# Two cross-attention layers on one core: maxima of the next block taken in the bank of the projections, keys and values computed at other places, and unread products on TensorE

## The reference

```python
q = split_heads(LN(x) @ Wq.T + bq) / sqrt(16)      # 16 heads of 16, 128 queries
k = split_heads(ctx @ Wk.T + bk)                   # 12544 keys
v = split_heads(ctx @ Wv.T + bv)
s = q @ k.T + (1 - mask) * -10000                  # first layer only: mask (128, 12544)
x = x + softmax(s) @ v                             # the second layer has another projection Wo, bo
```

## Time and profile before

| | |
|---|---|
| Median of 3 runs | 1091.87 us (1090.59 to 1091.94) |
| The profiled execution: time | 1094.2 us |
| The profiled execution: span, first to last instruction | 1092.5 us |
| TensorE busy | 1024.6 us, 94% of the span |
| VectorE busy | 743.1 us, 68% |
| ScalarE busy | 679.3 us, 62% |
| GpSimd busy | 420.0 us, 38%, nearly all in the first layer |
| Mean granted clock of TensorE | 0.975 |

### The profile page before, as it was taken

One profiled execution on the slowest core, in us unless ns is written; L12 is line 12 of the kernel. 1 busy time (PEld: TensorE's weight loads), 2 busy tenths in 40 slices (PEclk: granted clock), 3 DMA queues, 4 the chain that ended last, 5 costly groups with the idle time before them and its releaser, 6 DMA issues. The chain is left out here.

```text
span 1092.5 us, 30637 instructions
## 1 busy us (share of the span) xinstructions
PE 1024.6 (94%) x12851; PEld 687.2 (63%) x12851; DVE 743.1 (68%) x1714; ACT 679.3 (62%) x951; POOL 420.0 (38%) x374
## 2 busy tenths in 40 slices
PE   7899999999999999977878899999999999999877
PEld 4466666666666666655544576666666666666655
DVE  4788888888888888766347756655656555556555
ACT  3677777777778787765542555555655556555632
POOL 4268888888888888760100000000000000000000
PEclk9899999999999999998987999999999999999998
DMA  7410122201222012130031010111100111000000
GB/s 305 137 59 29 52 69 69 69 19 52 69 70 69 19 53 69 52 133 22 10 134 49 2 32 6 35 36 36 35 15 22 36 35 36 2 2 2 2 1 6
DMA packets 14682, 53.31 MB, mean 49 GB/s; under 512 B 3025, under 2 KB 4817, under 8 KB 13649
## 3 DMA queue, kind: packets, MB, share of 16 engines
q1 hardware_dynamic: 14544, 51.35, 13.6%
HBM read 51.21 MB, written 0.13 MB: 47 GB/s over the span
## 5 line engine op out<-in xcount | busy, mean ns | idle before, releaser
L740 DVE TENSOR_REDUCE tile_max<-ps_max 128x1 f32<-128x448 f32 x416 | 241.9, 620 | 161.1 <-PE ps_max L1054 159.7
L737 DVE CUSTOM_DVE_ANT_0 unread<-ps_max,masks 128x448 bf16<-128x448 f32 x432 | 253.5, 621 | 70.6 <-PE ps_max L1054 68.5
L413 POOL TENSOR_TENSOR probs<-probs,masks 128x512 f32<-128x512 f32 x182 | 227.8, 1273 | 77.9 <-ACT probs L526 76.9
L533 ACT ACTIVATE probs<-probs 128x1024 f32<-128x1024 f32 x196 | 207.4, 1058 | 58.7 <-DVE probs L795 46.7
L538 ACT ACTIVATE probs<-ps_scores 128x1024 f32<-128x1024 f32 x193 | 187.2, 1021 | 90.4 <-PE ps_scores L1095 90.3
L1095 PE MATMUL ps_scores<-q_pad,k_full 32*128 32x256 f32 x3088 | 233.9, 380 | 0.0
L1111 PE MATMUL ps_out<-probs,values 128*32 128x128 f32 x6272 | 214.9, 278 | 6.0 <-ACT probs L533 4.9
L1111 PEld LDWEIGHTS ps_out<-probs,values 128*32 128x32 f32 x6272 | 161.4, 111 | 58.8 <-issue 50.1
L1054 PE MATMUL ps_max<-k_high,q_high 32*128 32x448 bf16 x848 | 183.7, 360 | 14.0 <-DVE tile_max L740 7.6
L1095 PEld LDWEIGHTS ps_scores<-q_pad,k_full 32*128 32x128 f32 x3088 | 193.8, 188 | 1.0
L1042 PE MATMUL ps_proj<-ctx_t,wk 128*128 128x448 f32 x368 | 163.4, 567 | 0.0
(11 more groups left out here) (249 smaller groups left out, 787.7 us busy)
## 6 DMA issues: line engine op xcount, KB each, us to landing
ctx_t<-in_ctx_t SPq DMA_DIRECT2D x28, 896.0 KB, 5.3
masks<-in_mask_n SPq DMA_DIRECT2D x14, 448.0 KB, 3.4
masks<-in_mask_t SPq DMA_DIRECT2D x14, 448.0 KB, 3.6
room_w<-in_L_attn_f_w SPq DMA_DIRECT2D x2, 1024.0 KB, 8.9
room_w<-in_L_ffn_w SPq DMA_DIRECT2D x2, 1024.0 KB, 7.5
room_w<-in_L_ffn_w_gate SPq DMA_DIRECT2D x1, 1024.0 KB, 10.4
room_w<-in_L_ffn_w_up SPq DMA_DIRECT2D x1, 1024.0 KB, 12.9
room_w<-in_L_ffn_w_down SPq DMA_DIRECT2D x1, 1024.0 KB, 14.9
```

Of the source, the lines that this page charges most:

```text
L413: nc.gpsimd.tensor_tensor(p, p, three(mask_t[m % 2], TILES)[:, t, :].unsqueeze(1).to_broadcast([P, 4, P]), ALU.add).then_inc(sig("bias_add ...
L533: nc.scalar.activation(prob(T, half), prob(T, half), ACT.Exp).then_inc(sig(f"exp_done{half}"), 1)
L737: ins = v.tensor_tensor_reduce(unread[:, j % 2, :], max_bank(m, j)[:, 0:HALF], mask_n[m % 2][:, HALF * half:HALF * (half + 1)], 1.0, -3e38 ...
L740: ins = v.tensor_reduce(tile_max[:, h, half:half + 1], ps_max[:, j % 2, 0:HALF], AX_X, ALU.max)
```

## The change

**Maxima.** `ps_proj` becomes a third bank for them: where two stand behind the scores, the first goes to `ps_proj` (except at t = 1, where the sums are turned in it), all others take the banks of `ps_max` in turn. A table (`MAX_BANK`, `MAX_AFTER`) holds the bank of each and how many maxima must have been read before. In the blocks that are not the first of a layer, the counts change from 1 (t = 0, 2, 3, 4) or 0 behind the scores and 2 at every t behind the weighing, to 2 behind the scores (1 at t = 1, in the first layer at t = 3 also) and 2 behind the weighing at t = 1, 3, 5 only (1 at t = 5 in the second layer). The sum stays 32. Ahead of the next scores stand 2 as before.

**VectorE's order in the first layer:** the first maximum behind the scores, then the mask's addition, then the second.

**Keys and values.** The keys of block 14 move from the stage between the layers into block 12; one piece of values of block 15 stays beside the first maxima, the other three go between the layers, in another order.

**The gated feed-forward** is done in two halves (SiLU and the product with up), and SiLU's table is loaded ahead by a dummy activation.

**Unread products** are added: small ones at the start, 2 and 4 ahead of `turn_max` of a layer's first block, one behind each of ten pairs of maxima, one per tile from t = 2 in block 13 and 3 behind it, and 3 in the feed-forward.

```diff
-        EXTRA_AT = (0, 2, 3, 4)
-        LAST_AT = 5
+
+
+        ONE_AT = ((1, 3), (1,))
+        WEIGHED_AT = ({1: 2, 3: 2, 5: 2}, {1: 2, 3: 2, 5: 1})
+        LAST_AT, SUMS_AT = 5, 1
         def count_at(m, t):
-            n = m % NB
...
             now, ahead = (0, 0, 0), (0, 0, 0)
+            first, middle = 1 if t in ONE_AT[l] else 2, WEIGHED_AT[l].get(t, 0)
             if n + 1 < NB:
-                if t < LAST_AT:
-                    now = (2 if n == 0 else int(t in EXTRA_AT), 2, 2)
-                elif t == LAST_AT:
-                    now = (0, 2, 0)
+                if n == 0:
+                    now = (2, 2, 2) if t < LAST_AT else (0, 2, 0) if t == LAST_AT else now
+                elif t <= LAST_AT:
+                    now = (first, middle, 2 if t < LAST_AT else 0)
             if n + 2 < NB:
-                ahead = (0, 0, 2) if t == LAST_AT else (0, 2, 2) if t > LAST_AT else (0, 0, 0)
+                ahead = (0, 0, 2) if t == LAST_AT else (first, middle, 2) if t > LAST_AT else ahead
             return now, ahead
-        MAXIMA = {}
+
+        MAXIMA, MAX_BANK, MAX_AFTER = {}, {}, {}
...
+            done, read = {NB * l: 2 * H}, {bank: 2 * H * (NB * l + 1) for bank in range(2)}
+            turn_of = 0
             for m in range(NB * l, NB * (l + 1)):
                 for t in range(TILES):
...
                             here += [(to, j) for j in range(at, at + count)]
                             done[to] = at + count
+                        for i, (to, j) in enumerate(here):
+                            if k == 0 and len(here) == 2 and i == 0 and (t != SUMS_AT or m % NB == 0):
+                                MAX_BANK[to, j] = 2
+                            else:
+                                MAX_BANK[to, j], MAX_AFTER[to, j] = turn_of, read[turn_of]
+                                read[turn_of] = 2 * H * to + j + 1
+                                turn_of = 1 - turn_of
...
         def max_bank(m, j):
-            return (ps_max[:, j % 2, :], ps_scores[:, j % 2, :])[1 - j // 2 % 2 if m == 0 else 0]
-
-        def max_reuse(m):
-            return 4 if m == 0 else 2
+            if m == 0:
+                return (ps_max[:, j % 2, :], ps_scores[:, j % 2, :])[1 - j // 2 % 2]
+            return (ps_max[:, 0, :], ps_max[:, 1, :], ps_proj)[MAX_BANK[m, j]]
...
-        BETWEEN = [("k", NB, j) for j in range(4)] + [("k", NB + 1, j) for j in range(4)]
-        BETWEEN += [("v", NB, u) for u in range(PAIRS)] + [("k", NB + 2, j) for j in range(3)]
...
-        BESIDE = [("k", NB + 2, 3)] + [("v", NB + 1, u) for u in range(PAIRS)]
-        BESIDE_AT = (1, 4, 7, 10, 13)
+        BETWEEN = [("k", NB + 1, 0), ("k", NB + 1, 1), ("v", NB, 0), ("v", NB, 1), ("k", NB + 1, 2), ("v", NB, 2), ("k", NB + 1, 3),
+                   ("k", NB + 2, 0), ("v", NB, 3), ("v", NB + 1, 0), ("v", NB + 1, 1), ("v", NB + 1, 2)]
+        BETWEEN += [("k", NB + 2, 1), ("k", NB + 2, 2)]
+
+
+        BESIDE = [("k", NB + 2, 3), ("v", NB + 1, 3)]
+        BESIDE_AT = (1, 4)
         def keys_in_block(m):
-            return m < BLOCKS and m not in (NB, NB + 1, NB + 2)
+            return m < BLOCKS and m not in (NB + 1, NB + 2)
...
+                    act.wait_ge(sig("table_loaded"), 2)
+                    nc.scalar.activation(stat[:, 30:31], ones[:, 0:1], ACT.Silu).then_inc(sig("table_loaded"), 1)
...
-                    act.wait_ge(sig("gate_ready"), 1)
-                    nc.scalar.activation(gelu, ps_scores[:, 0:2, :].rearrange("p a n -> p (a n)"), ACT.Silu,
-                                         scale=stat[:, 20:21]).then_inc(sig("silu_ready"), 1)
-                    between_out(10, 11, 12, 13)
+                    for half in range(2):
+                        act.wait_ge(sig("gate_ready"), half + 1)
+                        nc.scalar.activation(gelu[:, 512 * half:512 * (half + 1)], ps_scores[:, half, :], ACT.Silu,
+                                             scale=stat[:, 20:21]).then_inc(sig("silu_ready"), 1)
...
-                        for k, j in behind_scores:
+                        for k, j in behind_scores[0:1 + l]:
                             maximum(k, j)
                         if l == 0 and is_last(m):
                             bias_last(m, t)
                         elif l == 0:
                             bias_first(m, t)
+                        for k, j in behind_scores[1 + l:]:
+                            maximum(k, j)
                         if t == SUMS_AT and n > 0:
                             add_sums(m - 1)
...
+                    for half in range(2):
+                        cols = slice(512 * half, 512 * (half + 1))
+                        dve.wait_ge(sig("gate_ready"), 3 + half)
+                        dve.wait_ge(sig("silu_ready"), 1 + half)
+                        note(v.scalar_tensor_tensor(out=big[:, cols], in0=ps_scores[:, 2 + half, :], scalar=stat[:, 21:22],
+                                                    in1=gelu[:, cols], op0=ALU.mult, op1=ALU.mult))
+                    dve.wait_ge(sig("dve_link"), links[0])
...
-                need("max_free", J + 1 - max_reuse(m))
+                if m == 0:
+                    need("max_free", J - 3)
+                elif MAX_BANK[m, j] == 2:
+                    proj_free(("max_free", J + 1))
+                else:
+                    pe.wait_ge(sig("max_free"), MAX_AFTER[m, j])
...
             pe.wait_ge(sig("idents"), 3)
+            idents(4)
...
                 if l == 0:
+                    idents(4)
...
                             beside_in(BESIDE_AT.index(i))
-                    for u in range(len(BESIDE)):
-                        beside_read(u)
+                        elif i > 5:
+                            idle_products(1, ps_out)
+                        if i == 5:
+                            for u in range(len(BESIDE)):
+                                beside_read(u)
                 read_by[0] = ("max_copied", NB * l + 1)
+                idle_products(2 + 2 * l, ps_proj)
...
+                        if m == NB - 1 and t > SUMS_AT:
+                            proj_free(None)
+                            idle_products(1, ps_proj)
                         for k, j in ahead:
                             maximum(k, j)
+                if l == 0:
+                    idle_products(3, ps_proj)
...
+                            last.then_inc(sig("gate_ready"), 1)
+                    between_in(10, 11, 12)
+                    idle_products(1, ps_proj)
...
+                    idle_products(2, ps_proj)
...
```

28 lines of the change are left out of this document (14 added, 14 removed).

## The result

The changed kernel takes 1098.86 us in the median, the kernel before, on the same chip, 1091.91. The ratio of their runs is 1.0055, 95% interval 1.0040 to 1.0069: 6 us slower by the ratio, 7 by the medians, where the forecast said 1095.8 and 3.9. The profiled execution took 1098.86 us with a span of 1097.1, the one of before 1094.2 and 1092.5.

What follows compares the result with a forecast made beforehand. TensorE was taken to bound the first layer, with VectorE close behind. Terms from +14.7 (blocks 1 to 11) to -6.4 (second layer) sum to +3.9 on 1091.87, giving 1095.8 us; own range 1091 to 1101, with rivals 1078 to 1107.

Steps and rivals of the forecast that it cites:

- t = 5 of the first layer: TensorE waits for a bank read only behind the mask; lent values begin at 4.25 instead of 2.87, +1.38 us a block.
- the wait isn't there: Rival: the bank at t = 5 is free in time, 1063 us; wait smaller or absent has chance 0.18.
- t = 6: First layer: turned maxima wait for a mask one maximum later, from 2.96 to 3.50 after the pair, +0.54 us.
- t = 1: First layer: a maximum comes ahead of the sums' addition and the values wait for that addition, +0.39 us.
- t = 0, 2, 4: First-layer tiles: the pair behind the weighing goes, worth 0.29, and the second maximum costs 0.02; -0.27 us each.
- Block 0: All five full tiles get the wait of t = 5, a tile of keys 5.96 instead of 4.92; +5.3 us.
- Blocks 12 and 13: Block 12's waits and half-clock stretches filled by keys, -1.5 us; block 13's products +0.9 against a faster clock, 0.
- Between the layers: SiLU in halves -1.2 us, shorter waits at the first pair maxima -2.5, low-clock slices 19 and 21 -1.5.
- Block 14's scores: Second layer's start: scores of 2.20 us at 1.2 GHz take about 1.1 at full clock, half counted, -1.5 us.
- The second layer: No mask stands between the reads; -0.53 us a block, -6.4 for twelve; block 26 -1.5, block 14 0.
- Clock lost: Rival: new waits at t = 5 and t = 6 bring the first layer's clock down; +12, 1108 us, chance 0.17.
- Clock gained: Rival: unread products and the filled block 12 keep the clock at 2.4 GHz from 440 on; 1088 us, chance 0.23.

Runs made afterwards that it cites:

- experiment 5: Changed kernel with one first-layer maximum moved from behind the scores at t = 5 to behind the weighing at t = 0; 1089.92 us in one execution.
- experiment 3: Changed kernel, but in the first layer VectorE reads both maxima behind the scores before adding the mask; 1109.53 us, ratio 1.0183 to the kernel before.
- experiment 7: Changed kernel with the first layer's new counts only at t = 0, 2, 4, the rest and block 0 as before; 1080.07 us, ratio 0.9889.
- experiment 12: Kernel of experiment 11 without block 13's five unread products; 1069.76 us, ratio 0.980 to the kernel before.
- experiment 10: Changed kernel without the unread products of block 13 alone; 1102.14 us in one execution.
- experiment 2: Changed kernel with the second layer's counts and banks of maxima as before; 1105.68 us, ratio 1.0122 to the kernel before.
- experiment 6: Changed kernel with VectorE adding the mask ahead of both maxima at t = 6 of the first layer alone; 1094.02 us in one execution.
- experiment 8: Changed kernel with the four pieces of block 14's keys back between the layers, ahead of the others; 1106.92 us, ratio 1.0157 to the kernel before.
- experiment 11: Changed kernel with the first layer's maxima as before and four more unread products in TensorE's waits; 1073.80 us, ratio 0.9857 to the kernel before.
- experiment 4: Changed kernel without the unread products that the change added; 1103.83 us, ratio 1.0116 to the kernel before.

## Why the prediction was right, step by step

**t = 5 of the first layer** (+1.38, lent values at 4.25): 4.18 after the pair, wait 1.14. Right in place and size. One part was missing: had the bank been free, the mask would have held the values until 3.42 (experiment 5) or, with both maxima ahead of it, 4.18 (experiment 3). So my rival "the wait isn't there", priced at 1063, left out what is late next: without the wait for the bank a block would have been shorter by 0.76 there at most, while the rival made the whole block 2.4 shorter.

**t = 6** (turned maxima at 3.50): 3.50. **t = 1** (+0.39): values at 3.76 after the pair with a wait of 0.39. **t = 0, 2, 4** (-0.27 each): t = 4 takes 4.09 against 4.39, -0.30. What a weighing followed directly by keys costs was open: in the changed kernel the keys begin 1.02 after the weighing does (277.16, 278.18), in experiment 7 a maximum begins 1.01 after it and the keys 0.29 later, so the pair was worth its whole 0.29. **t = 3** (-0.16): 4.61 for 4.77. **The block** 35.01 for 35.1; blocks 1 to 11 +13.6 for +14.7. **Block 0** +5.0 for +5.3: a tile of keys 5.89 for 5.96, and experiment 3, where block 0 takes 34.35 with the same work, shows that it is the order of VectorE's reads that sets those tiles and not their number. **The start** (0, between -2 and +1) was -1.6, but kernels with the changed start took 35.5 to 37.3, so no effect of the products there is shown.

**Blocks 12 and 13.** Block 12 -1.9 for -1.5, and its clock kept, as said. Block 13's products cost 1.2 to 1.3 (experiments 12 and 10), two tiles 6.60 in place of 5.97, where I had +0.9. That a faster clock pays it back holds for the changed kernel, but that these products make the clock faster is not borne out: experiments 10 and 12 keep it in block 13 without them, and experiments 2 and 6 have 3.4 us of low clock there (at 508 and 505) with them.

**Between the layers** (0 for block 13, -1.2, -2.5 and -1.5 for low slices, -5.2 in all) it was -6.3. VectorE's milestones of both traces, from one to the next:

| from, to | before | after |
|---|---|---|
| block 13's chain, first layer's result | 35.88 | 35.14 |
| linear attention's first addition | 10.05 | 9.58 |
| product behind SiLU | 27.22 | 25.96 |
| second layer's queries | 13.67 | 12.96 |
| first pair maximum | 2.91 | 2.91 |
| block 14's chain | 20.61 | 17.48 |

SiLU gave 1.26, as forecast; the pair maxima 3.1 where I had 2.5 (of the two waits of 3.8 together, 0.44 is left); the 1.2 of the second and fourth line go with low stretches that are gone. The size was right at the pair maxima, but I put it down to the moved pieces, and most of it goes with the clock. The piece beside the first pair was not moved: it took 3.02 at the lower clock and takes 1.77, and experiment 8, with the changed kernel's pieces there, has the long wait back (2.09) when its clock is low. The last piece of values, which was moved, took 3.60 at the lower clock, against 1.99 for such a piece at full clock. What its move alone gives has no run. The pieces of values that left the pair maxima now stand where the keys of block 14 stood, at no cost; with the keys there as well the stretch is 6.0 longer (experiment 8). My sum had the gain but not this condition for it. **Block 14's scores** (-1.5 of clock) failed: the scores at 604.99 took 2.20 as before, after the wait of 1.34 at 603.43. With two products in that wait (experiments 11 and 12, one trace each) the clock stayed up, which is what I had expected of the four ahead of `turn_max`; those stand before the wait and not in it.

**The second layer**: 0.52 a block for 0.53; experiment 2 shows that the counts alone do it. The sum was -6.7 for -9.4 with blocks 14 and 26: block 14 gave +0.6 by its clock, and block 15 and the last gave 1.2 each.

**The rest** +2.5 for 0, low clock in more stretches behind 1030 (0.89 over the last 83 us of the profiled execution, 0.94 before over 80). Of the twelve experiments, all with the same code there, nine took 79.5 to 80.8 from the last chain and three 82.4 to 82.9: it varies from execution to execution, so no effect of the change is shown in it.

**The rivals.** *Clock lost* is refuted: waits of 1.14 and 0.86 in each of eleven blocks left the granted clock at its upper level, 2.4 GHz, from 48 to 600. By the rule of the Trainium skill that I weighed (TensorE: Matmul & The Clock Gate, "A second HAM failure mode: psum-queue depth-cycling", short idle times between groups can make the clock swing) it could have swung here too; the trace shows none of it in these blocks, and the measurement decides. The other section that I named with it, "HAM oscillation", is about longer waits for transfers and does not bear on this. *Clock gained* came half true: stage and block 12 without a low stretch, block 14, block 0 and the rest with one. It could be had whole, in another kernel: the profiled execution of experiment 12 has a mean clock of 0.997.

That the sum came so near is partly luck. Its terms are off by -1.1 (blocks 1 to 11), -0.3 (block 0), -0.4 (block 12), -1.6 (the start), -1.1 (between the layers), +2.7 (the second layer) and +2.5 (the rest), and these cancel to less than 1. The part that carries the argument, the first layer's waits, is not luck: place and size were read from rows and found.

The median is 3.1 us above the forecast. Of that 0.8 lies in the profiled executions, 4.7 apart in place of 3.9. The other 2.3 is that I let the profiled execution stand as far above the median after the change as before it; it stood on the median. Where in the other executions those 2.3 us lie stays open, since only one execution of each kernel has a trace.

## What to carry to other kernels

A wait for a bank is set by where its read stands in the reader's order, so before moving a product, write down for each wait what the reader does ahead of that read, and then what would be late next if the wait were gone: here it was the mask, and of the 1.3 us lost at t = 5 only 0.76 could be had back by removing that wait. A short product between the weighing and the keys costs 0.29, be it one or two (the two begin together); only emptying the place gains. Unread products belong into the wait after which the clock fell, not ahead of it and not ahead of work that somebody waits for: five of them in block 13 cost 1.2 us and held nothing in these traces that was not held without them, two in one wait of block 14 went with 3.5 us less there than in the changed kernel (1.2 less than in the kernels whose clock was low for only 3.4 us). The second of these is read from the traces of experiments 11 and 12 alone, and three other executions of experiment 11 had a lower mean clock.

## What the runs showed of the hardware

The steady blocks repeat to 0.01 us: 32.47 in the second layer in the twelve kernels with its new counts, 33.74 in the first in five (only block 5 takes 0.34 more, in every kernel). What varies between the profiled executions is the stretches at 1.2 GHz, which all lie outside the steady blocks. After a wait of 1.34 (0.81 in experiment 2) for VectorE at its start, block 14 took 29.7 to 32.1, with 10 us and more at the lower clock, in seven kernels, and 27.3 to 27.5, with 3.4 us, in four others. In ten of the eleven the block's first tiles are the same but for the banks of experiment 2, and the clock fell between 4.6 and 5.7 us after the chain; in experiment 4, without the unread products, it was low already. So the clock fell in all of them, and what the same wait cost differed by 2 us and more.
